# Three DMAs of a graph network's kernel are issued at other points of SyncE's queue

## The reference

```python
h = maximum(layernorm(x), 0)
for W_l, W_r, b in layers:                    # two layers
    agg = segment_sum(h[src], dst) / maximum(count, 1)
    h = relu(agg @ W_l + h @ W_r + b)
x = x + h
h = maximum(layernorm(x), 0)
m = relu(concat([h[src], h[dst]]) @ W_interact + b_interact)
out = h + relu((h + segment_sum(m, src) / 4) @ W_update + b_update)
return x + out
```

## Time and profile before

| | us |
|---|---|
| median of 3 runs | 1552.71 |
| the runs | 1549.72 to 1559.3 |
| span of the profiled execution | 1552.8 |
| busy in it: PE | 1322.9 |
| DVE | 1343.5 |
| ACT | 940.1 |
| POOL | 931.1 |

### The profile page before, as it was taken

The page is one execution under the profiler, slowest core; times in us unless marked ns, Lnnn a source line. Parts: engine busy times, 40 slices in busy tenths (PEclk is TensorE's granted clock), DMA queues, the critical chain, the costliest instruction groups (busy, mean ns, idle before and its releaser), DMA issues.

```text
span 1552.8 us, 39671 instructions
## 1 busy us (share of the span) xinstructions
PE 1322.9 (85%) x14762; PEld 1128.6 (73%) x14762; DVE 1343.5 (87%) x3914; ACT 940.1 (61%) x1835; POOL 931.1 (60%) x942
## 2 busy tenths in 40 slices
PE   1512877999999989899999679889999999999997
PEld 1311655777777767677767578889899999998887
DVE  6968878999999945777866679999999999999998
ACT  2642766778777942010001358878888878887886
POOL 5253803777773005677770147777777777777773
PEclk9965889999999999999999789999999999999999
DMA  4003554475646218799987234444444444444442
GB/s 120 1 1 89 198 232 150 152 253 180 228 177 211 113 50 278 257 310 305 305 280 220 72 77 122 138 121 126 128 127 120 128 127 126 134 131 126 127 120 61
DMA packets 121785, 241.63 MB, mean 156 GB/s; under 512 B 20184, under 2 KB 74601, under 8 KB 121594
## 3 DMA queue, kind: packets, MB, share of 16 engines
q1 hardware_dynamic: 95179, 187.74, 36.1%
q0 software_dynamic: 24832, 50.78, 13.2%
q10 hardware_dynamic: 1584, 0.59, 0.1%
HBM read 169.09 MB, written 73.14 MB: 156 GB/s over the span
## 4 chain that ended last, share of the span: by engine, by line
PE 46%; DVE 35%; issue 7%; SPq 4%; DMA 4%; ACT 3%; POOL 2%; DVEq 1%; ACTq 0%; POOLq 0%
PE ps L1262 13%; PE ps L1468 12%; DVE room L2186 6%; PE ps L1244 5%; DVE hot L1809 4%; PE ps L1233 3%; PE ps L1479 3%; PE ps L1459 3%; DVE slab L2230 2%; SPq L663 2%; PE ps L1302 2%; DVE ps L2222 2%; DVE keys L1935 2%; DVE keys L1934 2%; DVE hot L1804 2%
## 5 line engine op out<-in xcount | busy, mean ns | idle before, releaser
L1014 ACT ACTIVATE slab<-ps 128x980 f16<-128x980 f32 x256 | 321.2, 1277 | 118.7 <-PE ps L1233 102.9
L925 POOL DMA_INDIRECT cells<-b_rows,work x236 | 245.1, 1039 | 74.9 <-issue 67.7
L1468 PE MATMUL ps<-slab,room 125*128 125x128 f16 x3538 | 236.0, 221 | 36.0 <-DVE room L2186 33.5
L1244 PE MATMUL ps<-slab,room 128*128 128x320 f16 x1568 | 252.2, 301 | 0.1
L1468 PEld LDWEIGHTS ps<-slab,room 125*128 125x128 f16 x3538 | 206.5, 98 | 49.5 <-DVE room L2186 49.1
L1123 ACT ACTIVATE lnw<-iota_w,keys 128x126 f32<-128x126 f32 x750 | 242.4, 389 | 0.0
L1459 PE MATMUL ps<-inv,hot 125*128 125x128 f16 x1800 | 224.3, 220 | 5.2 <-DVE hot L2176 5.1
L1262 PE MATMUL ps<-slab,room 128*128 128x320 f16 x1568 | 226.9, 301 | 0.0
L1233 PE MATMUL ps<-hot 128*128 128x245 bf16 x1024 | 160.6, 282 | 50.4 <-DVE hot L1809 39.0
L889 POOL DMA_INDIRECT hot<-t_rows,pairs x160 | 165.8, 1036 | 55.2 <-issue 48.1
L1262 PEld LDWEIGHTS ps<-slab,room 128*128 128x128 f16 x1568 | 153.2, 98 | 59.4 <-issue 2.7
(11 more groups left out here) (371 smaller groups left out, 2442.4 us busy)
## 6 DMA issues: line engine op xcount, KB each, us to landing
slabs_d<-slab SPq DMA_DIRECT2D x14, 3920.0 KB, 13.9
slab<-slabs_d SPq DMA_DIRECT2D x98, 560.0 KB, 5.5
hot<-lane_d SPq DMA_DIRECT2D x50, 576.0 KB
inv<-inv_row SPq DMA_DIRECT2D x32, 160.0 KB, 7.0
keys<-up_d SPq DMA_DIRECT2D x25, 160.0 KB
room<-up_d SPq DMA_DIRECT2D x25, 160.0 KB
cells<-b_rows,work POOLq DMA_INDIRECT x236
t_rows<-room SPq DMA_DIRECT2D x1, 3200.0 KB, 13.7
```

The lines of the kernel that those rows point to most:

```text
L925: p.indirect_dma_start(rows_g[gi % RS][:, j, :], None, b_rows, bass.IndirectOffsetOnAxis(ap=node_t[:, t:t + 1], axis=0)).then_inc(e_gath[g ...
L1014: a.activation(slab[par][:, :, u * UB * BW:(u + 1) * UB * BW].rearrange("p h (k d) -> p k h d", k=UB), psum_unit(u).rearrange("p k (h d) - ...
L1244: last = t.matmul(ps[:, 4 + s % 2, 0:SC], table[:, h, term, :], slab[s % 2][:, h, :], start=k == 0, stop=k == HI * HALVES - 1)
L1468: last = t.matmul(to, end_hot[g // 3][0:BN, u:u + P], bt[0:BN, bt_at(tile, w), k, :], start=False, stop=w == w1 - 1 and k == HALVES - 1)
```

## The change

The copy of the input rows is issued directly after the loads of `x0`, with a wait for the weights ahead of it. The store of the table's rows no longer waits for the inverse counts and stands before their store. The load of the tail's inverse counts is issued in slab 3, after the load of that slab's counts and before the wait for the slab's eviction, and no longer in slab 4.

```diff
             for p0, p1 in LAST_ROWS:
                 sp.dma_start(x0[p0:p1, N // P, :], x[FULL + p0:FULL + p1, :]).then_inc(s_x[1], 16)
 
+            sp.wait_ge(s_w, 16 * 11)
+            sp.dma_start(a_rows.rearrange("(t p) f -> p t f", p=BN), x.rearrange("(t p) f -> p t f", p=BN)
+                         ).then_inc(s_first, 16)
             sp.wait_ge(s_lim_row, 2)
...
             sp.dma_start(lim[:, :, :], lim_d.rearrange("l (p f) -> p l f", f=FH)).then_inc(s_lim, 16)
+            sp.wait_ge(PS_[0]["t_lo"], NC)
+            sp.dma_start(t_rows[0].rearrange("(t p) f -> p t f", p=P), table.rearrange("p t k n -> p t (k n)")
+                         ).then_inc(l_store[0], 16)
             sp.wait_ge(c_inv, 1)
             sp.dma_start(inv_row.rearrange("(j p k) -> p j k", p=P, k=BW), icnt[:, :, :]).then_inc(s_irow, 16)
             sp.wait_ge(s_irow, 16)
-            sp.wait_ge(PS_[0]["t_lo"], NC)
-            sp.dma_start(t_rows[0].rearrange("(t p) f -> p t f", p=P), table.rearrange("p t k n -> p t (k n)")
-                         ).then_inc(l_store[0], 16)
-            sp.dma_start(a_rows.rearrange("(t p) f -> p t f", p=BN), x.rearrange("(t p) f -> p t f", p=BN)
-                         ).then_inc(s_first, 16)
...
             for s in range(NS):
-                if s == DECODED_AT[0] + 1:
+                load_inv(0, s)
+                if s == DECODED_AT[0]:
                     sp.wait_ge(AS[0]["hot"], DECODED_AT[0] * SU + DECODED_AT[1] + 2)
                     load_tail_inv(0)
-                load_inv(0, s)
                 sp.wait_ge(AS[0]["evict"], min(s * SU + SU, UNITS) + PRE)
```

## The result

The changed kernel takes 1544.12 us (median of 5 runs, 1542.66 to 1545.15), the kernel before beside it 1552.98 (5 runs, 1549.72 to 1559.3). The ratio is 0.9935 with a 95% interval of 0.9916 to 0.9953, a gain of 10.1 us (7.3 to 13.0). The ratio is taken over all the runs and is not that of the two medians, which lie 8.9 us apart. The span of the changed kernel's profiled execution is 1542.3 us, 10.5 less than before's 1552.8.

The account below looks back on a forecast made before the run. DVE and PE had room; the bound was stretches where both stand still, behind SyncE's queue and its transfers. Gains 8.6 + 9.0 + 0 + 0 = 17.6 us; 1552.8 - 17.6 = 1535.2 us, range 1530 to 1546.

Parts of the forecast that it names:

- its signs: In the profile after: copy issued near 21.4, slab 0's store near 164, ACT's DMA wait and DVE's tail wait gone.
- rival B: At the tail's unit DVE still stops, for the first tail sum or gathers, despite the early load; 1544.2 us, chance 0.14.
- Term 1: From slab 0's store to slab 2: ACT's stop goes and PE keeps full clock; 8.6 us gained (4 to 9.03).
- Term 2: At the tail's inverse counts: DVE's 6.35 us wait goes, its wait for PE falls by 2.65; 9.0 us (0 to 9.3).
- The early copy: Copy issued at about 21.4 us, beside the DVE chain to 136 us; cost taken as 0 (bounds 0 and 32.11).
- the sum of 63.3: On SyncE's queue the limits go out at 21.4 + 9.75 + 32.11 = 63.3 us, over 70 us before DVE reads them.
- Rival E: Code loads queue behind the early copy on DVE's chain, 21 to 136 us, up to 32 us; 1567 us, chance 0.06.
- The early store of the term rows: Store issued at 90.4, over before 110 us; cost through contention on SBUF or DVE taken as 0, bounds 0 and 1.
- The reference point: Start of the forecast: profiled span 1552.8 us set beside the runs' median 1552.7, so no correction; good to some 3 us.
- C: Slab 0's store takes twice as long, 28.6 us, beside gathers, so Term 1 is 5.6; 1538.2 us, chance 0.08.
- D: The two waits hid others, on the clock or between DVE and PE; 0 to 3 us left, 1551 us, chance 0.06.
- the gain is carried to the end: From 274.5 us on nothing holds to a fixed time, so the whole gain of 17.6 us reaches the kernel's end.

Follow-up runs that it names:

- e2: Kernel before with only the copy of the input rows and the store of the term rows moved; 1547.72 us, ratio 0.9953.
- e4: Changed kernel with the store of the term rows back behind the inverse counts; 1536.8 us, ratio 0.9879.
- e7: Changed kernel with the copy back behind the inverse counts and the store of the term rows after the placements, at 113.78 us; 1539.59 us, ratio 0.9898.
- e8: Kernel before with only the copy's shape changed, to long pieces in 128 equal parts and 16 for the rest; 1545.95 us, ratio 0.9948.
- e1: Kernel before with only the load of the tail's inverse counts moved to slab 3; 1547.52 us against 1555.58, ratio 0.995.
- e3: Changed kernel with the store of the term rows issued only after all placements, at 114.19 us; 1537.13 us, ratio 0.9887.
- e12: The kernel of e4 again, in another set of runs; 1541.1 us against 1552.67, ratio 0.992.
- e10: The unchanged kernel before, measured against itself; ratio 1.001.
- e11: The changed kernel unaltered, a third time, on the same chip as e10; 6.5 us below before (4.1 to 9.0).
- e9: Changed kernel with the copy at about 88 us, in 512-byte pieces on 128 partitions, and the store of the term rows behind the inverse counts; one run, 1543.13 us.

## Why the prediction was right, and where it was not

The forecast was 1535.2 us, the result 1544.12, inside the range of 1530 to 1546. The direction and both terms were right. The gain was forecast at 17.6 us and measured at 10.1 (7.3 to 13.0): 3.1 of the missing 7.5 can be named, the other 4.4 can't. The largest chance, 0.58, stood on a kernel faster by over 1%, and it is faster by 0.65%. The prediction's own test says wrong on both counts: its signs hold and the end didn't move by 15 us, and DVE's way from 21 us to the inverse counts did grow (21.53 to 136.44 before, 19.29 to 137.17 after, 3.0 us more). The median happens to be rival B's 1544.2, which is luck, since B did not happen: its wait would stand at the tail's unit, and in DVE's timeline after, the row of 250.55 stands without one.

**Term 1** was forecast at 8.6 us and measured 8.7. ACT's stop went, the clock stayed at 2.4 GHz from 189 to 205 us (1.00), and DVE's wait fell to 0.32 us. Elsewhere the clock did not stay up: from 220 to 225 us it was 0.72, where before it was 1.00 from 215 to 235, but DVE was busy for 4.93 of these 5 us and lost nothing. e2 shows term 1 without the third edit. The reason given, two transfers ahead of the store, was complete but wider than needed: by e4 and e7 one of the two had to leave, and by e8 none.

**Term 2** was forecast at 9.0 and measured 8.9, alone in e1 as well. PE's slow piece went with DVE's wait, and the rest, 0.47 us, was forecast at 0.3.

**The early copy** was taken at 0, and is. It was issued at 18.74, not 21.4, since ACT's first use of the weights was only a bound for their arrival, and held the limits for 27.28 us, for which DVE never waited. Its own issue took 0.93 us there and in e7, not the 9.75 that the sum of 63.3 counted: those were the hold behind the store of the term rows, as the 9.64 us of e4's load show. Rival E, loads of code held up behind it, did not occur: from the statistics to the placements DVE took 71.97 us against 72.11.

**The early store of the term rows** is the step that failed, a term that the sum put at 0: "A cost through contention on SBUF or DVE I bound by 0 and 1 us". It cost 3.1 us in every profile that had it at 88 us (25.49 to 25.55 against 22.35 to 22.37 in the ones that did not). I bounded it by DVE's busy time beside other traffic in 154 to 183 us, where DVE has no idle time "until issue" and where no store out of SBUF ran (that of the term rows had landed at 154.36, that of slab 0 went out at 183.01), and did not look at what DVE does from 90 to 116: 26 placements, each behind a load of a register. A timeline of DVE from 90 to 105 us would have shown it: one short copy in every 0.73 us, and idle time "until issue" between them. e3 and e4 take this cost away and come to 17.6 and 18.8 us below before in their set of runs, near the 17.6 that was forecast for the changed kernel; but e12, the kernel of e4 again, came to 12.4.

**The reference point** compares two different things: "so no correction is made" sets a span beside a time. An execution's time is 1.8 or 1.9 us above its span (1544.12 and 1542.3 after, 1557.57 and 1555.7 in e10), so the profiled execution of before took some 1554.6 by estimate. That the 1552.8 it started from agrees with the median of before, 1552.98, is luck, and it did the forecast no harm.

**Rivals C and D.** Slab 0's store landed 13.5 us after its issue at 164.96, so C did not occur, although POOL issued twenty gathers from 146.20 to past 185 us (the first 8.5 us earlier than before) and five of them began while the store ran. That "most of them are over when the store begins" was too much, since ten were, and it did not matter. C's own sum is off as well: 192.9 is 3.8 us after 189.13, not 3, so its term 1 would be 4.8. D expected 0 to 3 us and falls.

The rest, 4.4 us, has no cause that a run here shows. In the profile it lies behind 294.46 us, in stretches that differ from one execution to the next as much as between the kernels; for the other runs of the first result there is no profile, and e11 shows that the rest can be larger (8.5 us). "From 274.5 on all engines go by each other [...] the gain is carried to the end" holds for the first layer (16.9 us at 274, 16.4 at 878 us) and isn't shown for the edge part.

## What to carry to other kernels

An engine that idles "until issue" can be at work all the same, here on loads of registers that no row counts as busy: before a transfer is moved beside such a stretch, look at what the engines do there, and keep stores out of SBUF away from it, as far as one such store can tell. When a queue stops for tens of microseconds, look first at the shape of the transfer ahead of the held issue; changing that (e8) gave the same as moving two transfers. And undo each part of a change that worked by itself: one of three parts here brought nothing and cost 3 us.

## What was not expected of the hardware

- A register load from SBUF took longer while the store of the term rows read SBUF: 1.00 us in place of 0.30 on DVE, and 1.43 in place of 0.73 for the step of load and placement, beside 269 GB/s; it was unchanged beside a copy from DRAM to DRAM of 329 GB/s (e9).
- The issue behind a DMA of thousands of 512-byte pieces is held for most of that DMA's duration, even if it is a small load: 32.11 us before, 27.28 after and 30.14 in e7 behind the copy on 125 rows, 9.64 behind the store of the term rows (e4), 8.63 behind the copy on 128 rows (e9), but 0.69 behind the copy in long pieces (e8).
- The gain of one kernel over another differs between sets of runs by more than its intervals (6.5 to 12.7 us for the changed kernel), though the profiled stages agree to 1 us. The sets were on different chips.
